# Routed experts and state space layer put into one block of a decoder kernel

## The reference, cut to what matters

```
x = layernorm(x + self_attention(x))          # layer 0
x = layernorm(x + cross_attention(x, ctx))
x = layernorm(x + experts(x))                 # 2 of 8 routed experts, and a shared one
x = layernorm(x + state_space(x))             # layer 1
x = layernorm(x + cross_attention(x, ctx))
x = layernorm(x + lora_experts(x))
```

```
z, xBC, dt = split(x @ W_in.T)                # 512, 768 and 8 columns
xBC = silu(conv4(xBC) + conv_b)               # 4 taps along the 64 tokens
x, B, C = split(xBC)                          # 128, 128 and 512 columns
dt = softplus(dt + dt_bias)                   # the time widths, 8 per token
```

## Time and profile before

| | us |
|---|---|
| median of 3 runs | 1277.18 |
| the runs | 1277.14 to 1280.21 |
| the profiled execution, its own time | 1271.43 |
| its span | 1269.6 |
| TensorE busy | 1113.0 |
| VectorE busy | 781.1 |
| ScalarE busy | 575.6 |
| GpSimd busy | 459.7 |

### The profile page before, as it was taken

How to read it: one execution, slowest core, us unless ns; L and a number is a source line. 1 busy time by engine, 2 the same in 40 slices (tenths; PEclk the granted TensorE clock), 3 DMA queues, 4 the chain that set the end, 5 groups by cost and what they waited for, 6 DMA issues and landing times. The chain is left out here.

```text
span 1269.6 us, 20983 instructions
## 1 busy us (share of the span) xinstructions
PE 1113.0 (88%) x7484; PEld 662.9 (52%) x7484; DVE 781.1 (62%) x1521; ACT 575.6 (45%) x1199; POOL 459.7 (36%) x702
## 2 busy tenths in 40 slices
PE   5898869898898578999579998789998899999997
PEld 3566535444453245776224455567876343545455
DVE  2999887888884322332667677735566365555554
ACT  2666516667667301333456654356765332122120
POOL 8999851544542264333224445421111000000001
PEclk9999979999999799999689999989999899999999
DMA  6657354556552023333324000000000000000000
GB/s 212 202 173 258 93 134 114 142 142 151 142 138 56 25 80 96 106 108 99 105 65 141 1 1 1 1 1 2 2 2 1 26 1 0 9 9 9 8 9 26
DMA packets 72844, 91.72 MB, mean 72 GB/s; under 512 B 12676, under 2 KB 61470, under 8 KB 72062
## 3 DMA queue, kind: packets, MB, share of 16 engines
q1 hardware_dynamic: 68323, 80.72, 22.6%
q0 software_dynamic: 3408, 9.34, 2.1%
q10 hardware_dynamic: 1010, 0.31, 0.1%
HBM read 55.37 MB, written 29.17 MB: 67 GB/s over the span
## 5 line engine op out<-in xcount | busy, mean ns | idle before, releaser
L910 ACT ACTIVATE a_late<-a_qkv 128x512 f32<-128x512 f32 x128 | 77.3, 604 | 59.0 <-PE a_qkv L987 59.0
L2537 POOL TENSOR_SCALAR f_rstd<-f_mv 128x1 f32<-128x1 f32 x16 | 3.7, 230 | 266.7 <-DVE f_mv L2676 266.6
L858 DVE TENSOR_REDUCE b_nm<-a_s 128x4 f32<-128x1024 f32 x64 | 78.0, 1219 | 29.5 <-PE a_s L956 29.4
L2621 DVE TENSOR_TENSOR f_prod<-f_sg,f_kept 128x512 f32<-128x512 f32 (+1 forms) x48 | 33.2, 692 | 96.4 <-ACT f_kept L2566 93.5
L2746 PE MATMUL fps_h<-residT,w_f_w 128*128 128x512 f32 x176 | 82.4, 608 | 2.5 <-DVE f_inner L2658 2.5
L858 DVE TENSOR_REDUCE b_nm<-a_pt 128x4 f32<-128x1024 f32 x64 | 76.7, 1198 | 2.2 <-PE a_pt L956 2.2
L910 ACT ACTIVATE a_late<-a_y 128x512 f32<-128x512 f32 x128 | 77.0, 602 | 0.0
L2560 ACT ACTIVATE f_sg<-fps_h 128x512 f32<-128x512 f32 (+1 forms) x24 | 14.3, 596 | 125.2 <-PE fps_h L2765 108.3
L1002 PE MATMUL a_o<-a_late,b_vt 128*32 128x256 f32 x1024 | 69.3, 389 | 0.0
L1290 POOL DMA_INDIRECT routed<-c_out,c_target x39 | 37.4, 959 | 67.3 <-ACT c_out L1362 67.0
L1879 DVE SCALAR_TENSOR_TENSOR d_acc<-d_pad,d_cw,d_acc 128x512 f32<-128x512 f32 x72 | 57.7, 809 | 1.7
(11 more groups left out here) (425 smaller groups left out, 2903.0 us busy)
## 6 DMA issues: line engine op xcount, KB each, us to landing
kparts<-a_rest SPq DMA_DIRECT2D x48, 192.0 KB, 3.1
a_rest<-a_rest SPq DMA_DIRECT2D x64, 128.0 KB, 3.0
xrows<-in_c_fill SPq DMA_DIRECT2D x13, 387.0 KB, 4.1
c_xrow<-xrows SPq DMA_DIRECT2D x39, 129.0 KB
c_back<-routed SPq DMA_DIRECT2D x16, 256.0 KB, 3.3
a_front<-kparts SPq DMA_DIRECT2D x12, 288.0 KB
a_front<-qparts SPq DMA_DIRECT2D x36, 96.0 KB
qparts<-b_xp SPq DMA_DIRECT2D x48, 64.0 KB, 2.8
```

The lines of the kernel that those rows point to most:

```text
L858: dve.tensor_reduce(nm[s % 2][:, 4 * n:4 * n + 4].rearrange("p (g h) -> p g h", h=2), s1[step % 2][:], AX.X, ALU.max, negate=True).then_in ...
L910: act.activation(pr[g % 8][:], s2[g % 2][:], ACT.Exp, scale=SCALE).then_inc(s2_out, 1)
L2621: dve.tensor_tensor(prod[n % 2][at], sg[n % 2][at], up, ALU.mult).then_inc(prod_done, 1)
```

## The change

`layer0_experts` no longer runs a block of its own. It hands its five lists of instructions to `layer1_state_space` as functions that take a callback `between`, and one block holds both. Barriers two and three are gone, and so is the end of the block before them. Semaphores are cleared by `release`, on GpSimd alone, behind the barrier of the block that ends ahead of the experts (one clear) and of the one that ends behind the state space layer (two clears). PSUM banks of the experts are used again by the state space layer. The order of the experts' weights in memory and in the queue is another one.

```
-        self.nc.all_engine_barrier()
-        self.nc.clear_and_free_semaphores(self.sems)
-        self.nc.all_engine_barrier()
...
+            for c in range(NCHUNK):
+                for t in range(TPC * c, TPC * (c + 1)):
                     turn_back(t)
+                between(pe, c)
...
+                def between(sp, s):
+                    if s == 12:
+                        for dst, src in dt_consts:
+                            sp.dma_start(dst[:], io[src]).then_inc(dt_const, 16)
+                    elif s == 14:
+                        for dst, src in conv_consts:
+                            sp.dma_start(dst[:], src).then_inc(conv_const, 16)
+                    elif s == 16:
+                        sp.dma_start(wz[:], io["d_win"][:, :, XT * P:]).then_inc(gate_const, 16)
+                    elif s in (18, 20, 22):
+                        for dst, src in consts[s - 18:s - 16]:
+                            sp.dma_start(dst[:], io[src]).then_inc(const, 16)
...
+                def between(act, c):
+                    if c == -1:
+                        act.wait_ge(dt_const, 16 * len(dt_consts))
+                        act.activation(an[:], alog[:], ACT.Exp).then_inc(an_exp, 1)
+                    elif c == 0:
+                        act.wait_ge(conv_const, 16 * len(conv_consts))
+                        act.wait_ge(padded, 4)
+                        evacuate(own[0])
+                        evacuate(own[1])
+                    elif c == 1:
+                        evacuate(own[2])
+                        evacuate(own[3])
+                    elif c == 2:
+                        act.wait_ge(const, 16 * len(consts))
+                        for g in range(G):
+                            ins = act.activation(wout[:, g, :], wout[:, g, :], ACT.Copy, scale=nw[:, g:g + 1])
+                        ins.then_inc(wout_done, 1)
...
+                act.wait_ge(lt_full, NCHUNK)
                 act.activation(ltT[:], lt_ps[:], ACT.Copy).then_inc(lt_out, 1)
                 act.wait_ge(ab_done, 1)
                 act.activation(e[:], ab[:], ACT.Exp, scale=-1.0).then_inc(e_done, 1)
-                for n in own[:4]:
-                    evacuate(n)
-                decay(0)
                 activate(("in", 0, 0))
...
+                experts.vector(dve)
...
                 dve.scalar_tensor_tensor(out=dt[:], in0=p_[:], scalar=2.0, in1=x[:], op0=ALU.mult, op1=ALU.add).then_inc(dt_done, 1)
...
+                for n in own:
+                    convolve(n)
                 time(0)
...
+                def step_inputs(c):
+                    if c == 0:
+                        pe.wait_ge(dt_const, 16 * len(dt_consts))
+                    for kd in range(KD):
                         ins = pe.matmul(lt_ps[32 * c:32 * c + 32, :], wdt[:, kd, :], k.residT[:, kd, c * CHUNK:(c + 1) * CHUNK],
                                         start=(kd == 0), stop=(kd == KD - 1))
+                    ins.then_inc(lt_full, 1)
...
+                def between(pe, c):
+                    pe.wait_ge(left.rT_out, TPC * (c + 1))
+                    if c < 3:
+                        for n in own[2 * c:2 * c + 2]:
+                            fill(n)
+                    step_inputs(c)
```

More of the change, by code:

```diff
@@ new lines, in sync @@
+        def sync(sp, between):
+            for n in range(2):
+                sp.wait_ge(scattered[n], 16 * TILES)
+            for s in range(XSLOTS):
+                if s >= 4:
+                    sp.wait_ge(x_turned, s - 3)
+                    sp.wait_ge(target_done, s - 3)
+                sp.dma_start(xrow[s % 4][:], k.xrows[s * P:(s + 1) * P, :]).then_inc(x_in[s % 4], 16)
+                between(sp, s)
+            for v in range(4):
+                sp.wait_ge(sent[v], 16 * len(range(v, XSLOTS, 4)))
+            for h in range(2 * NCHUNK):
+                c, half = divmod(h, 2)
+                if h >= 2:
+                    sp.wait_ge(back_in[h % 2], 32 * (h // 2))
+                if h >= 4:
+                    sp.wait_ge(r_done, 2 * (h - 3))
+                for n in range(2):
+                    first = n * NTOK + h * 2 * P
+                    sp.dma_start(back[n][c % 2][:, 2 * half:2 * half + 2, :], routed[first:first + 2 * P, :].rearrange("(t p) f -> p t f", p=P)
+                                 ).then_inc(back_in[h % 2], 16)
@@ L1608, in _ @@
+            for c in range(EARLY, NCHUNK):
+                for m in range(MS):
+                    shared_up(c, m)
+                shared_down(c)
+            for c in range(NCHUNK):
+                for t in range(TPC * c, TPC * (c + 1)):
                     turn_back(t)
+                between(pe, c)
+    k.second = Programs(sync, gpsimd, scalar, vector, tensor), Left(h_ps, o_ps, t_ps, x_ps, sdown, rT_out)
 def layer1_state_space(k):
@@ L1623, in layer1_state_space @@
     SLOTS = TILES + 7
+    experts, left = k.second
     jobs, slot_jobs = [], {}
@@ L1936, in mean_square @@
                     dve.tensor_scalar(ms[q % 2][:], ss_ps, 1.0 / P, EPS, ALU.mult, ALU.add).then_inc(ms_out, 1)
+                experts.vector(dve)
+                own = [n for n in slot_jobs[-1] if jobs[n] in nth and jobs[n][1] == 0]
+                dve.wait_ge(conv_const, 16 * len(conv_consts))
                 st = Steps(dve, pre, 0)
@@ L2079, in _ @@
                 ins.then_inc(dt_full, 1)
-                own = [n for n in slot_jobs[-1] if jobs[n][1] == 0]
-                for n in own[:4]:
-                    fill(n)
+                fill(own[6])
+                fill(own[7])
                 pe.wait_ge(const, 16 * len(consts))
                 segments(0)
-                for n in slot_jobs[-1][4:]:
+                for n in slot_jobs[-1][8:]:
                     fill(n)
@@ L2169, in layer1_cross_attention @@
         SLOTS = TILES + 6
+        k.release(old)
         def live(t):
```

710 lines of the change are left out of this document (336 added, 374 removed).

## The result

| | runs | median us | range | ratio to before, 95% interval |
|---|---|---|---|---|
| before | 6 | 1277.16 | 1274.71 to 1281.55 | |
| changed | 6 | 1287.57 | 1279.49 to 1288.57 | 1.006, 1.0033 to 1.0087 |
| changed once more (`e1_again`) | 12 | 1287.51 | 1279.31 to 1292.19 | 1.0051, 1.0026 to 1.0076 |

The changed kernel is slower, by 0.3 to 0.9% (the interval of the second row). The ratios are the recorded ones, each against the runs of before beside it, and not the quotients of the medians: those of the first two rows would give 1.008, and beside `e1_again` before had a median of 1278.58. The forecast was 1283.7 with a range from 1276 to 1289. The sign and the place were right; what was given a chance of 0.17 (rival B, on top of the forecast) came as well.

A forecast was written before the change was run, and what follows sets the result against it. The prediction took VectorE's and GpSimd's work to bound the tail, and TensorE's idle joint as the place to gain. Tail and joint -0.1, order +1.85, clock +4.75 gave +6.5 us: 1277.18 to 1283.7, range 1276 to 1289.

The forecast's parts named there:

- rival B: End of the state space block: GpSimd's long drain is paid there, +3.4 us on top of the forecast, 1287; chance 0.17.
- The tail and the joint: Up to VectorE's first step: 9.7 us put into the tail use up what the joint gave, -0.1 us.
- A lone pair of narrow products: Experts' tail, TensorE: one chunk's two narrow products alone take 1.75 us at the full clock.
- Rival C: Tail: narrow products are cheap alone, 1.3 us less for each of two pairs; 1276.3 with the clock up; chance 0.07.
- The order ahead of products(0): Behind the last convolution: last activation, an evacuation and two fills make 4.85 us where it was 3.0, +1.85.
- VectorE's 23.2 us: Steps of the time widths, then all six convolutions: order and 23.2 us stay the same.
- The clock: Tail, TensorE at half clock: +1.7 first fill, +2.55 as half of three more drops, +0.5 slow turns; +4.75 in all.
- Rival A: Tail: the clock stays up or comes back at once, +1.75 to +3.5 us, about 1279.5, no change; chance 0.22.
- the signs: Expected in the trace: `apply` of chunks 1, 2, 3 near 621, 630, 639; VectorE's first step at 645 to 650.
- The other joint: Behind the state space layer: GpSimd's two clears with drains, 2.3 us, stay hidden with 0.5 us to spare.
- The slots behind `products(0)`: From `products(0)` to the end: the slots are the same, so the +6.5 us there carries through.
- Rival D: Tail: the added work hides in the gaps, -8 us, 1269; chance 0.09.

The follow-up runs named there:

- e1_again: The changed kernel run once more without an edit, beside the kernel before: 1287.51 us median of 12, ratio 1.0051.
- e3_behind: Changed kernel with the six fills and four evacuations moved out of the tail, behind the turn of the time widths: 1278.51 us, ratio 0.9982.
- e6_old_order: Changed kernel with TensorE's and ScalarE's old order behind the tail, narrow products between chunks, and an early GpSimd drain: 1270.47 us, ratio 0.9936.
- e4_order: Changed kernel with ScalarE's last activation moved behind the evacuations of the last two z jobs: 1286.95 us, ratio 1.0066.
- e8_pipelined: Changed kernel with one fill per gap, evacuated one gap later, narrow products behind the tail, three jobs convolved early, wout's scaling moved, early drain: 1264.49 us.
- e10_drains: Changed kernel with four more GpSimd drains: one before the indirect transfers, one behind the first 32, two behind the next 39: 1281.98 us, single time.
- e9_before: The kernel before, run once more without an edit: 1276.22 us, single time.
- the second group: Four kernels, among them `e1_again` (1287.51 us), on one chip with the kernel before (1278.58 us).
- e2_drain: Changed kernel with one more GpSimd drain behind the last scatter of the experts: 1284.93 us, ratio 1.0042.

## Why the prediction was right, and what it missed

**The tail and the joint: -0.1 us. Right.** The stretch from the shared product to the first step took 37.66 us before and, with the full clock, 37.66 in `e1_again`. What the joint gave was used up exactly. `e3_behind` and `e6_old_order` show the other side: without the fills the step stands 5.3 and 6.3 us earlier.

**A lone pair of narrow products costs as much as a full one, 1.75. Right:** 1.90, and 3.57 at the lower clock. Rival C falls. Between the chunks it cost the path nothing all the same, since TensorE did it while ScalarE evacuated: in chunk 1 it ended at 622.59 + 1.90 = 624.49, and `apply` of the first tile at about the same time. It stood on the path ahead of chunk 3's turns, as forecast, and behind the last copy.

**The order ahead of products(0): 4.85 instead of 3.0. Right:** 4.84. I had put all of the +1.85 down to the last activation. `e4_order` shows 0.63 for that; the rest came back only where the decay of tile 0 also stood further ahead of the last activation (`e8_pipelined` 2.45, `e6_old_order` 3.77 with the low stretch named above). Both were in the order that I had read. The split between them is argued from the table loads and not measured by itself.

**VectorE's 23.2 us "are the same": wrong by 0.8.** From first step to last convolution it was 22.4 in the change and in `e1_again`. The steps took 6.05 instead of 6.87; the section on the hardware says why. So `products(0)` came 1.0 later in `e1_again` than before, where +1.75 was reckoned for the full clock.

**The clock: +4.75. The mechanism was right, the size a matter of chance.** 0 to 6.8 us in eight tails, 3.6 on average. In the profile on record it was all four places, 6.6 (three pairs of fills at 1.65 and the last narrow pair at 1.67); the +0.5 for slow turns did not come, the turns of that tail ran at the full clock. Rival A (+1.75 to 3.5 in all, clock full) describes three of the eight. The sentence that needed care was the one about the half: it is no property of the kernel. For the same reason two of the signs lay outside what was said for them: the first step stood at 653.04 and not at 645 to 650, and `apply` of chunk 2 at 634.10 and not near 630 (1.85 of each is the later start of the tail).

**The other joint: "Hidden, with 0.5 us to spare". This is the step that failed.** It looked at the clears and memsets that `release` puts ahead of the next block, and took the drain at 0.338 from a row of a block that had had no indirect transfers. The drain of 6.17 moved to this joint, as rival B had it, with its 3.4 us: the joint took 6.45 us instead of 3.08. The reason given against it, that the transfers lie 200 us back, does not count: the drain took 6.17 us both 30 and 240 us behind the last of them, and `e10_drains` shows that its length goes by their number.

**The slots behind `products(0)`.** "The same": they are, within the scatter. From `products(0)` to the end of the state space layer's last product (cross less `products(0)` less last joint) it took 158.6 and 163.5 us in the two profiles of before, and 160.8, 163.0 and 158.2 in the three of the change.

**Sum.** Tail 3.6 on average, order 1.85, less 0.3 to 0.8 for the steps (6.3 us in `e9_before`, 6.87 in the first profile, 6.05 in the change), drain 3.4: 8.1 to 8.6. The forecast of +6.5 had 1.2 us more for the clock than this average, 0.3 to 0.8 too much for the steps, and nothing for the drain's 3.4. That it lies only some 2 us under this sum is partly luck. The medians of the second group differ by 8.9, and those of the first runs by 10.4; the ratios put it at 6.5 to 7.7. Two things stay open. From the first product of the last block (`fps_o<-residT,w_f_gw`) to the end, the two profiles of before show 281.4 and 281.3 us and the twelve of kernels with one block 281.4 to 285.8; two profiles of before are too few to say whether that is chance. And the part ahead of the experts' tail took 605 to 616 us in the merged kernels, 610 on average, and 607 and 608 before; the new order of the weights, which I had costed at nothing, was not undone alone, nor were the constants in the experts' loop.

**Rival D** (fills hidden in gaps) falls for two fills a gap, as forecast, and holds for one: `e8_pipelined`.

## What to carry to other kernels

When two phases are merged, the work that is pulled forward must fit into the waits that it is put into, results included: two fills in a gap of two microseconds cost what the barrier had cost, and with one fill and its evacuation a gap later the first step stood where it stood with no fill at all (31.46 and 31.35). Then ask who takes up the early result: here VectorE, idle for 20 us, still did the late steps first, and turning its list brought `products(0)` 7 us forward. A cost that a barrier pays (a drain behind indirect transfers) goes to the next barrier when that one is removed; pay it by hand where the engine is idle.

## What the runs showed of the hardware

The length of GpSimd's drain grew with the indirect transfers since the last drain: 0.13 us each in `e10_drains` (4.12 / 32, 4.88 / 39), 0.11 for all 71 at once in `e2_drain` (7.51 / 71), 0.09 when it came 30 us later, in the kernel before, or 240 us later, in the changed one (6.17 / 71). So the number is not all of it: two drains cost 9.0 us together where one cost 7.5.

A small step of VectorE stood still beside a GpSimd product. In the kernel before, `TENSOR_SCALAR` of L1956 took 1.05 us where the same form takes 0.23 (L1944). The two timelines of before, VectorE and GpSimd:

```profile
644.94 0.23 DVE L1944 TENSOR_SCALAR d_q<-d_x 128x128 f32<-128x128 f32 x1
...
647.77 1.05 DVE L1956 TENSOR_SCALAR d_p<-d_q 128x128 f32<-128x128 f32 x1
```

```profile
647.70 1.04 POOL L1748 TENSOR_TENSOR d_ddiag<-d_dd,d_eye 128x512 f32<-128x512 f32 x1 [7.56 <-DMA d_nw<-in_d_nw]
```

The change had moved GpSimd's product (`d_ddiag`) into the tail. Held back again until VectorE's third step:

> The changed kernel with one GpSimd instruction held back: the product of D and the unit matrix (128x512, 1.04 us) waits until VectorE has made the third of the steps of the time widths. In the kernel before it started at 647.70, and one small step of VectorE beside it took 1.05 us where its like takes 0.23; in the changed kernel it ran in the tail, and the steps took 6.05 instead of 6.87. If the two engines stand in each other's way, one of VectorE's small steps takes about 1 us again and the steps take 6.5 to 6.9. If the 0.82 had another cause, they stay at 6.05.

```profile
649.42 0.90 DVE L1986 TENSOR_SCALAR d_s<-d_e 128x128 f32<-128x128 f32 x1 [0.38 <-ACT d_e L1871]
```

```profile
649.19 1.04 POOL L1773 TENSOR_TENSOR d_ddiag<-d_dd,d_eye 128x512 f32<-128x512 f32 x1 [21.82 <-DVE d_ab L1984]
```

0.90 us for a step of 0.23, both done within 0.1 us of each other, and 6.72 for all the steps (the single time was 1283.84). In `e9_before` the same product began at 647.72, and beside it lay other steps: a reciprocal kept its 0.95 us, and the one behind it took 0.57 where it takes 0.29 in the first profile. The steps took 6.3:

```profile
648.34 0.57 DVE L1952 TENSOR_TENSOR d_s<-d_s,d_e 128x128 f32<-128x128 f32 x1
```

The Trainium skill (SBUF — State Buffer, on who interferes with whom) says that VectorE and GpSimd share a pair of ports for some instructions, `tensor_scalar` among them, and that the one that comes second waits for the whole of the other's. The traces agree, with 1.05 and 0.90 us for the `TENSOR_SCALAR` beside a product of 1.04.
